# Strassen operand sums of a GNN kernel: x sums pair by pair from quarters, weight sums in three buffers

## The chip, the cores and the metric

The kernel runs on one core of a Trainium2 chip. Its engines each run a program of their own and meet at semaphores: PE multiplies matrices, ACT and DVE work elementwise on tiles and on PE's results, POOL (GpSimd) does elementwise work beside them, and SP does nothing here but issue DMAs in the order of its program. The metric is device time of one launch in microseconds (us), lower is better.

## The reference, cut to what matters

1250 nodes with 1024 features go through four graph layers on one edge list (10000 random edges both ways, and the self loops); each layer is `x = layernorm(x + layer(x))`. What the change touches are the products of x or of a layer's input with a 1024 x 1024 weight matrix in float32:

```python
# layer 0: x1 = x @ W1 + b1, then four gated graph steps on 512 columns
for kk in range(4):
    alpha = tanh(x_i @ gw[:x.shape[1]] + x_j @ gw[x.shape[1]:] + gb)
    gnn_out = gnn_out + segment_sum(norm[:, None] * alpha * x_j, col)
# layer 1: two SAGE layers, relu between them
h = relu(x @ W_self0 + (segment_sum(x[src], dst) * deg_inv) @ W_neigh0 + b0)
out = h @ W_self1 + (segment_sum(h[src], dst) * deg_inv) @ W_neigh1 + b1
# layer 2: attention; h = x @ W, e = exp(-leaky_relu(al[src] + ar[dst]))
out = elu(segment_sum(e * h[dst], src) / (rowsum + EPS))
# layer 3: GCN
out = relu(segment_sum((x @ W)[src] * norm, dst) + b)
```

## The kernel before

**Tiles and turns.** Nodes are cut into NT = 10 tiles of T = 125. schedule() (L89) lists 325 jobs, JOBS, and every engine's program is one loop over the turns j, in which it does its part of job j and of some jobs ahead: PE the matmuls of job j, ACT first() and DVE second() the operands of a job one or two turns on, SP loads of jobs three to four turns on. The jobs in order: x1 (10), the gates of layer 0 (4 x 10), then for each SAGE layer a product with the self weights ("self", 35 jobs), one with the neighbour weights ("zq", 25 and later 10 more jobs) and the graph sums ("mean", 10 and 10 half jobs); then attention (z, att, kept), the last product (zq of layer 4, 25 and 10 jobs) and its graph sums ("loop").

**Quarter products.** A self or zq product is not done as one matrix product but, for each pair of row tiles (HT = 5 pairs, tile i and tile i + 5), as seven quarter products in the manner of Strassen and Winograd, one per phase: P1, P2, P4, P6, P7, P5, P3 for self, P1, P2, P6, P7, P4, P5, P3 for zq, five jobs each. Each multiplies a quarter of x (128 x 500, as 4 pieces of 128 x 125) or a sum of quarters with a quarter of W (512 x 512) or a sum of quarters. P1, P2 and P4 use plain quarters of x; P6, P7, P5 and P3 use sums (X_SUM): with x in quarters x11, x12, x21, x22, P5 takes S1 = x21 + x22, P6 S1 − x11, P7 x11 − x21, P3 x12 − (S1 − x11). P4 to P7 use sums of W (W_SUM). The numbers are float32 split into a high and a low part (xh, xl and wh, wl), so a quarter product is 4 x 3 matmuls, L1126 to L1128.

**x on its way.** SP's load(j) (L937) brings a quarter to one of four half buffers of xs at turn j − 4; ACT's first() makes xh (L1399), DVE xl (L1762), and PE's first matmul of the job, L1126, waits for xl. Weight slabs (128 x 512) come by stage() (L818) from W or, for the sums, from ws_d in memory; ACT L1389 and DVE L1749 split them.

**The sums.** sums_schedule() (L442) lists the steps (turn, kind, product, index) in one row. All go through two large buffers in turn, PW: U3F and XB (in the rows U and XO), four quarters each. A step at turn t: SP's step_load at t − 1 (two DMAs of 512 KB; L864 for weights, L876 for x), four POOL operations in four_sums at t (L2426 to L2432 for weights, L2434 to L2440 for x), SP's step_store at t + 2 (1 MB, L883 to ws_d or L885 to xs_d), which waits for the last of the four (semaphore s_sums). The load of step n waits for the store of step n − 2 to have landed. The job's own load then reads the sum back from xs_d. The weight steps of the first product stand in the gates from turn 14 on, the x steps at the first ten turns of self1, self2 and zq4, the other weight steps in the stages of products, 2 or 3 turns apart.

```python
for n in STEP_STORE.get(j, []):    # SP, turn j
    step_store(n)
for i in LOAD_AT.get(j, []):
    load(i)
for g in STAGE_AT.get(j, []):
    stage(g)
for n in STEP_LOAD.get(j, []):
    step_load(n)
```

**Around it.** In the gates SP loads the adjacency block Ar (L962), the rows R that are added (L910) and stores ul_d (L967); POOL turns the variances of a finished tile into 1/sigma by six small operations (soon(), L2355 to L2412). In the turns of self's P5 and P3, store_right (L895) stores 125-row halves to sr_d, two buffers in turn. For mean and loop jobs, DVE's second() makes the low part of an operand (L1773 signals it) at the start of turn j − 1, in front of post() of that turn, and PE's L1270 waits for it. In "mean", second half, of layer 2 DVE also makes the two attention sums of a tile (L2003, L2006).

## Time and profile before

| | us |
|---|---|
| median of 3 runs | 1686.04 (1683.31 to 1690.53) |
| the profiled execution | 1690.04 |
| its span | 1688.2 |
| PE busy | 1521.5 (90%) |
| DVE, ACT, POOL busy | 1033.9, 800.0, 404.4 |

By stage, with the spans in which the trace has them: gates 0 and 1 from 112.9 to 265.9 us, gates 2 and 3 to 413.4, self1 to 558.9, zq1 to 657.4, mean1 to 706.9, the rest of zq1 to 737.1, mean1's second half to 789.8, self2 to 923.7, zq2 to 1025.0, mean2 and the rest of zq2 to 1101.1, mean2's second half to 1176.6, attention to 1442.3, zq4 to 1541.5, loop4 to 1620.2 and its second half to 1688.2.

A group's row reads: line, engine, operation, output and inputs, count, then busy time and mean, then the idle time of the engine ahead of these instructions and what ended it. A wait is named by what came last. In a row of the chain of waits, "DMA a<-b" is the time from the issue of a transfer to its landing; a name with q (SPq, DVEq) is the engine's instruction queue.

### The profile page before, as it was taken

To read this page: it belongs to the slowest core of one execution; us is meant where nothing else is said; L and a number is where in the kernel's file an instruction comes from. 1 tells how busy PE (TensorE), PEld (TensorE's weight loads), DVE (VectorE), ACT (ScalarE), POOL (GpSimd) and SP (SyncE) were. 2 spreads that over 40 slices of the span, in tenths; PEclk is the share of its full clock that TensorE was granted. 3 is DMA by queue.
4 is the path that set the end of the run, shared out by engine and by line. 5 is a ranking of instruction groups with operands and counts; after the bars stand their busy time and mean duration, and the time that the engine had idled before them with its cause. 6 is when DMAs were issued, how large, how long until landed. Compare 5 with 4: busy or idle time off the path is not lost.

```text
span 1688.2 us, 19851 instructions
## 1 busy us (share of the span) xinstructions
PE 1521.5 (90%) x6685; PEld 1203.4 (71%) x6685; DVE 1033.9 (61%) x1652; ACT 800.0 (47%) x1498; POOL 404.4 (24%) x457
## 2 busy tenths in 40 slices
PE   8999999999678869999779779987999999879997
PEld 6877778788456647877557558766788778657775
DVE  9878898876347445554446455556589356245655
ACT  7676657677223324544123324344487246433332
POOL 0111252434443130001451320012144013320012
PEclk9999999999889989999889889998999999989998
DMA  5343374248987664547986664356656247783435
GB/s 193 112 156 105 109 239 140 95 145 283 315 280 250 234 214 159 191 151 231 288 301 233 233 212 130 127 177 231 197 161 201 92 169 273 254 261 124 143 91 176
DMA packets 152564, 324.03 MB, mean 192 GB/s; under 512 B 27202, under 2 KB 67772, under 8 KB 149896
## 3 DMA queue, kind: packets, MB, share of 16 engines
q1 hardware_dynamic: 139486, 283.87, 51.9%
q10 hardware_dynamic: 12970, 38.77, 6.0%
q8 instruction: 61, 1.00, 0.2%
q14 instruction: 47, 0.39, 0.1%
HBM read 221.76 MB, written 100.82 MB: 191 GB/s over the span
## 4 chain that ended last, share of the span: by engine, by line
PE 41%; DMA 24%; DVE 13%; ACT 8%; POOL 6%; issue 5%; SPq 2%; ACTq 1%; DVEq 0%; POOLq 0%
PE bank L1259 8%; PE bank L1263 6%; PE bank L1261 6%; DMA Ar<-a_d 5%; DMA xs_d<-U 3%; DMA sr_d<-U 3%; PE bank L1095 3%; PE bank L1096 3%; PE bank L1097 3%; DMA xs<-xs_d 3%; PE bank L1270 3%; PE bank L1126 2%; PE bank L1127 2%; PE bank L1128 2%; ACT Tt L1434 2%
## 5 line engine op out<-in xcount | busy, mean ns | idle before, releaser
L1259 PE MATMUL bank<-Zh,Mh 125*125 125x512 f32 x990 | 401.0, 405 | 3.5 <-DVE Zl L1831 3.2
L1126 PE MATMUL bank<-wh,xh 128*125 128x512 f32 x700 | 299.7, 428 | 114.4 <-DVE xl L1762 99.1
L1762 DVE TENSOR_TENSOR xl<-xs,xh 128x500 fp32r<-128x500 f32 (+1 forms) x205 | 168.7, 823 | 340.8 <-ACT xh L1399 339.0
L1399 ACT CAST xh<-xs 128x500 fp32r<-128x500 f32 (+1 forms) x205 | 137.0, 669 | 412.8 <-DMA xs<-xs_d 185.1
L1127 PE MATMUL bank<-wl,xh 128*125 128x512 f32 x700 | 291.9, 417 | 0.0
L1128 PE MATMUL bank<-wh,xl 128*125 128x512 f32 x700 | 290.9, 416 | 0.0
L1126 PEld LDWEIGHTS bank<-wh,xh 128*125 128x125 f32 x700 | 140.4, 201 | 167.9 <-issue 126.7
L1270 PE MATMUL bank<-Zl,Mh 125*125 125x512 f32 x590 | 238.5, 404 | 19.6 <-DVEq L1773 19.5
L1259 PEld LDWEIGHTS bank<-Zh,Mh 125*125 125x125 f32 x990 | 187.3, 189 | 49.6 <-ACT Zh L1469 4.1
L1128 PEld LDWEIGHTS bank<-wh,xl 128*125 128x125 f32 x700 | 139.8, 200 | 36.9
L1127 PEld LDWEIGHTS bank<-wl,xh 128*125 128x125 f32 x700 | 140.9, 201 | 33.1
L1263 PE MATMUL bank<-Zh,Ml 125*125 125x512 f32 x400 | 158.8, 397 | 4.0 <-DVE Ml L1776 4.0
L1261 PE MATMUL bank<-Zl,Mh 125*125 125x512 f32 x400 | 158.0, 395 | 0.0
L2355 POOL TENSOR_TENSOR mv<-mv,half 125x1 f32<-125x1 f32 x39 | 38.9, 998 | 492.4 <-DVE mv L1953 492.4
L1270 PEld LDWEIGHTS bank<-Zl,Mh 125*125 125x125 f32 x590 | 112.4, 191 | 51.9 <-issue 25.5
L1434 ACT ACTIVATE Tt<-PB,Q 125x125 f32<-125x125 f32 x400 | 120.8, 388 | 1.9 <-ACT XO L1546 1.9
L1749 DVE TENSOR_TENSOR wl<-Tt,wh 128x512 fp32r<-128x512 f32 x94 | 81.9, 871 | 49.9 <-ACT wh L1389 49.9
L1416 ACT CAST Mh<-Ar 125x1250 fp32r<-125x1250 int16 x60 | 74.2, 1236 | 77.8 <-DMA Ar<-a_d 41.4
L1416 ACT CAST Mh<-Tt 125x1250 fp32r<-125x1250 f32 x53 | 65.7, 1239 | 67.9 <-DVE Tt L1790 64.4
L1095 PE MATMUL bank<-wh,xh 128*125 128x512 f32 x232 | 95.9, 413 | 1.7 <-ACT xh L1399 1.2
L1096 PE MATMUL bank<-wl,xh 128*125 128x512 f32 x240 | 95.3, 397 | 0.0
L1097 PE MATMUL bank<-wh,xl 128*125 128x512 f32 x240 | 94.5, 394 | 0.0
(228 smaller groups left out, 2567.4 us busy)
## 6 DMA issues: line engine op xcount, KB each, us to landing
Ar<-a_d SPq DMA_DIRECT2D x100, 312.5 KB, 3.0
xs<-xs_d SPq DMA_DIRECT2D x100, 250.0 KB, 5.3
x_d<-XO ACTq DMA_DIRECT2D x30, 512.0 KB, 4.4
R<-x_d SPq DMA_DIRECT2D x60, 256.0 KB
xT_d<-XT ACTq DMA_DIRECT2D x30, 500.0 KB, 4.0
Tt<-ws_d SPq DMA_DIRECT2D x52, 256.0 KB, 5.7
xs<-xT_d SPq DMA_DIRECT2D x45, 250.0 KB, 6.2
ws_d<-U SPq DMA_DIRECT2D x10, 1024.0 KB, 4.9
```

What stands on the lines that cost most here:

```text
L1095: te.matmul(o, xh[b][:, k, :], wh[s][:], start=(k == 0), stop=False)
L1096: te.matmul(o, xh[b][:, k, :], wl[s][:], start=False, stop=False)
L1097: m = te.matmul(o, xl[b][:, k, :], wh[s][:], start=False, stop=(k == 7))
L1126: te.matmul(o, xh[b][:, 4 * h + k, :], wh[s][:], start=(k == 0 and not onto), stop=False, skip_group_check=True)
L1127: te.matmul(o, xh[b][:, 4 * h + k, :], wl[s][:], start=False, stop=False, skip_group_check=True)
L1128: m = te.matmul(o, xl[b][:, 4 * h + k, :], wh[s][:], start=False, stop=(k == 3), skip_group_check=True)
L1259: te.matmul(o, Mh[i][:, s, :], zh, start=(n == 0), stop=False)
L1261: te.matmul(o, Mh[i][:, s, :], zl, start=False, stop=False)
L1263: m = te.matmul(o, Ml[i][:, s, :], zh, start=False, stop=(n == NT - 1))
L1270: m = te.matmul(o, Mh[i][:, s, :], zl, start=False, stop=(n == NT - 1))
L1434: m = ac.activation(t[:, s, :], PB[:, d, :], ACT.Tanh, bias=PQ[k % 2][1][:, s:s + 1])
L1762: ve.tensor_tensor(xl[b][:, part, :], xs[b][:, part, :], xh[b][:, part, :].bitcast(f32), ALU.subtract) \
```

## The change

x sums. The four-quarter steps for x are gone, and so is xs_d4. For each row pair there are now four small sums, S1, P6, P7 and P3, listed in XSUMS. SX holds S1 (five buffers, four in XB and one in GW), SM the others (five: UF0, UF1 and three quarters of GW). SP's sum_load brings the quarter or quarters two turns ahead of the POOL operation (three for S1 in layers 1 and 2), pair_sum on POOL makes the sum three turns ahead of its job in one operation (two for P3), and ACT and DVE read it where it is (x_of), without a load of their own. In layers 1 and 2 sum_store writes each quarter to xs_d two turns later, since the zq jobs still read the sums from there; a place of SM is loaded again when that store has landed (place_free). The loads of jobs that need another quarter go one turn earlier, five ahead.

Weight sums. A step now has a place, a load turn, four turns for its four operations and a store turn; there are three places, U3F, XB and GW. The first product's steps stand in gates 2 and 3 instead of 0 to 2; zq1's and zq2's stand over some thirty turns each, and self2's in the second half of layer 1's mean.

Two more edits: the two loads of attention's row vectors into GW go from turn 51 to turn 87, and DVE's second() for mean and loop jobs from tile 2 on stands in lower() of the turn before, behind post() of the turn before that.

```diff
-        LOAD_AT.setdefault(_j - (4 if _job.kind in ("att", "self", "zq") else 3), []).append(_j)
+        LOAD_AT.setdefault(_j - (5 if _job.phase in X_SUM and (_job.kind == "self" or _job.layer == 4) else
+                                 4 if _job.kind in ("att", "self", "zq") else 3), []).append(_j)
...
-    steps = [(J0[0] + 4 + 6 * k, "w", 0, k) for k in range(4)]
-    at = {p: find(*p, phase="P1") for p in PRODUCTS}
-    steps += [(at["self", 1] + 2 * i, "x", 1, i) for i in range(HT)]
-    steps += [(at["self", 1] + 11 + 2 * k, "w", 1, k) for k in range(4)]
...
+    g, z = LAST_GATE, START["self", 1]
+    steps = [(1, g - 16, (g - 15, g - 14, g - 13, g - 12), g - 11, 0, 0),
+             (0, g - 13, (g - 11, g - 10, g - 9, g - 9), g - 8, 0, 1),
+             (2, g - 8, (g - 7, g - 7, g - 6, g - 6), g - 5, 0, 2),
+             (0, g - 6, (g - 5, g - 5, g - 4, g - 4), g - 3, 0, 3),
+             (0, g - 2, (g - 1, g - 1, g, g), z, 1, 0),
+             (2, g - 3, (z, z + 1, z + 2, z + 3), z + 4, 1, 1),
+             (0, z + 3, (z + 5, z + 6, z + 7, z + 8), z + 9, 1, 2),
+             (0, z + 12, (z + 14, z + 15, z + 16, z + 17), z + 18, 1, 3)]
...
+XSUMS = []
+for _p in (("self", 1), ("self", 2), ("zq", 4)):
+    for _i in range(HT):
+        XSUMS.append((START[_p] + (6 + 3 * _i // 2 if _p[0] == "self" else 3 + _i), _p[1], "S1", _i))
+    for _f in ("P6", "P7", "P3"):
+        for _i in range(HT):
+            XSUMS.append((find(*_p, _i, phase=_f) - 3, _p[1], _f, _i))
...
+    XSUM_LOAD.setdefault(_t - (3 if _f == "S1" and _layer < 3 else 2), []).append(_n)
+    if _layer < 3:
+        XSUM_STORE.setdefault(_t + 2, []).append(_n)
...
+            def place_free(n):
...
+                    sum_made(q, *XSUMS[o][1:])
+                    if layer < 3 and XSUMS[o][2] != "S1":
+                        sum_stored(q, *XSUMS[o][1:])
+                        q.wait_ge(s_xl, XI[find("self", layer, i, phase=XSUMS[o][2])] + 1)
...
                 for i in LOAD_AT.get(j, []):
                     if i >= 2:
                         load(i)
+                for n in XSUM_LOAD.get(j, []):
+                    sum_load(n)
                 for g in STAGE_AT.get(j, []):
                     stage(g)
+                for n in XSUM_STORE.get(j, []):
+                    sum_store(n)
...
-                    q.wait_ge(d_xs[X_SLOT[j]], 16 * X_NTH[j])
+                    if sum_of(j) is None:
+                        q.wait_ge(d_xs[X_SLOT[j]], 16 * X_NTH[j])
+                    else:
+                        q.wait_ge(s_sx, sum_of(j) + 1)
...
-                    elif JOBS[i].kind in ("gate", "att", "kept"):
+                    elif JOBS[i].kind in ("gate", "att", "kept") or JOBS[i].kind in ("mean", "loop") and JOBS[i].d >= 2:
                         second(i)
...
+                j = find("self" if layer < 3 else "zq", layer, i, phase=f)
+                sum_made(q, layer, "S1", i)
...
+                if f == "P6":
+                    po.tensor_tensor(o, SX[i], o, ALU.subtract).then_inc(s_sx, 1)
+                    return
...
-                for n in STEP_AT.get(j, []):
-                    four_sums(n)
+                for n in XSUM_AT.get(j, []):
+                    pair_sum(n)
+                for n, m in STEP_AT.get(j, []):
+                    weight_sum(n, m)
```

SP at the start of self1, before: x steps (L876 loads, L885 stores), x loads (L937) and weight slabs (L818).

```order
L876 DMA XO<-xT_d1 128x2x500 [waits s_tt,d_xo0,d_xo1,d_ps1]
L876 DMA XO<-xT_d1 128x2x500 [waits d_xt0]
L885 DMA xs_d1<-U3 512x1x500 [waits s_sums]
L937 DMA xs1<-xT_d1 128x500 [waits s_xl]
L818 DMA ws0<-ws_d0 128x512 [waits s_wl]
L937 DMA xs1<-xT_d1 128x500 [waits s_xl]
L818 DMA ws1<-ws_d0 128x512 [waits s_wl]
L876 DMA U3<-xT_d1 128x2x500 [waits d_ps0]
```

SP in self1 where the sums of P6 are stored and those of P7 loaded, after: L1051 is sum_store, L1041 the load of a quarter for a sum, L1106 the job's load, L932 the slab; d_sq counts landed sum stores, s_sx sums made.

```order
L1051 DMA xs_d1<-GW 128x500 [waits d_sq0]
L1051 DMA xs_d1<-U0 128x500 [waits d_sq1,s_sx]
L1106 DMA xs0<-xT_d1 128x500 [waits s_xl]
L1041 DMA U0<-xT_d1 128x500 [waits d_sq1]
L932 DMA Tt1<-ws_d0 128x512 [waits s_wl]
L1051 DMA xs_d1<-U1 128x500 [waits d_sq2,s_sx]
L1106 DMA xs0<-xT_d1 128x500 [waits s_xl]
L1041 DMA U1<-xT_d1 128x500 [waits d_sq2]
L1051 DMA xs_d1<-GW 128x500 [waits d_sq3,s_sx]
L1106 DMA xs1<-xT_d1 128x500 [waits s_xl]
```

The 1 MB stores and their four-quarter loads are replaced by a store and a load of one quarter per turn; from the fourth row on a load into U0, U1 or GW stands behind the landing of the store from the same place, and the slab of a later job stands behind that.

POOL at the start of self1, before:

```order
L2434 TENSOR_TENSOR U3<-U3 128x500 [waits d_pl0]
L2436 TENSOR_TENSOR U3<-U3 128x500 [waits s_own_p]
L2438 TENSOR_TENSOR U3<-U3 128x500 [waits s_own_p]
L2440 TENSOR_TENSOR U3<-U3 128x500 [waits s_own_p]
L2434 TENSOR_TENSOR XO<-XO 128x500 [waits d_pl1]
L2436 TENSOR_TENSOR XO<-XO 128x500 [waits s_own_p]
L2438 TENSOR_TENSOR XO<-XO 128x500 [waits s_own_p]
L2440 TENSOR_TENSOR XO<-XO 128x500 [waits s_own_p]
```

POOL in self1 in the turns ahead of P6 and P7, after: L2630 makes a P6 sum, L2634 a P7 sum, L2604 to L2608 are operations of a weight step.

```order
L2630 TENSOR_TENSOR U0<-XO,U0 128x500 [waits s_sx,d_sm0]
L2630 TENSOR_TENSOR U1<-XO,U1 128x500 [waits s_sx,d_sm1]
L2630 TENSOR_TENSOR GW<-XO,GW 128x500 [waits s_sx,d_sm2]
L2604 TENSOR_TENSOR U3<-U3 128x512 [waits d_pl0]
L2630 TENSOR_TENSOR GW<-XO,GW 128x500 [waits s_sx,d_sm3]
L2606 TENSOR_TENSOR U3<-U3 128x512 [waits s_own_p]
L2630 TENSOR_TENSOR GW<-GW 128x500 [waits s_sx,d_sm4]
L2608 TENSOR_TENSOR U3<-U3 128x512 [waits s_own_p]
L2634 TENSOR_TENSOR U0<-U0,xs0 128x500 [waits d_xs0,d_sm0]
L2610 TENSOR_TENSOR U3<-U3 128x512 [waits s_own_p]
L2634 TENSOR_TENSOR U1<-U1,xs0 128x500 [waits d_xs1,d_sm1]
```

Four dependent operations on one buffer have become one per sum, with the weight operations one by one between them.

POOL in gate 3, after (L2533 to L2590 are soon(), before L2355 to L2412, which stood there alone):

```order
L2590 TENSOR_SCALAR mv<-mv 125x1 [waits s_own_p]
L2604 TENSOR_TENSOR U3<-U3 128x512 [waits d_pl0]
L2606 TENSOR_TENSOR U3<-U3 128x512 [waits s_own_p]
L2533 TENSOR_TENSOR mv<-mv,half 125x1 [waits s_post]
L2535 TENSOR_TENSOR mv<-mv 125x1 [waits s_own_p]
L2537 TENSOR_TENSOR mv<-mv 125x1 [waits s_own_p]
L2539 TENSOR_SCALAR mv<-mv 125x1 [waits s_own_p]
L2541 TENSOR_TENSOR mv<-mv 125x1 [waits s_own_p]
L2590 TENSOR_SCALAR mv<-mv 125x1 [waits s_own_p]
L2608 TENSOR_TENSOR U3<-U3 128x512
L2610 TENSOR_TENSOR U3<-U3 128x512 [waits s_own_p]
```

Two operations of a weight step now stand behind the small ones of each of two turns.

## Rows read from the trace of the kernel before

**Rows 1.** The page, part 1: engine, busy us, share, instructions.

```profile
PE 1521.5 (90%) x6685; PEld 1203.4 (71%) x6685; DVE 1033.9 (61%) x1652; ACT 800.0 (47%) x1498; POOL 404.4 (24%) x457
```

**Rows 2.** Groups by line on PE: busy us, mean ns, idle before, releasers.

```profile
L1126 PE MATMUL bank<-wh,xh 128*125 128x512 f32 x700 | 299.7, 428 | 114.4 <-DVE xl L1762 99.1 <-ACT xh L1399 11.0 <-issue 3.9
...
L1270 PE MATMUL bank<-Zl,Mh 125*125 125x512 f32 x590 | 238.5, 404 | 19.6 <-DVEq L1773 19.5
```

**Rows 3.** Windows on PE: stretch, us, busy (count), clock, DMA share, GB/s.

```profile
112.90:265.90 153.00, 146.44 (x625) 0.98 0.46 154
265.90:413.40 147.50, 146.25 (x665) 1.00 0.48 161
413.40:558.90 145.50, 115.67 (x454) 0.89 0.83 279
558.90:657.40 98.50, 78.35 (x302) 0.90 0.57 199
737.10:789.80 52.70, 50.41 (x232) 1.00 0.67 207
789.80:923.70 133.90, 109.81 (x433) 0.91 0.82 274
923.70:1025.00 101.30, 80.10 (x301) 0.88 0.57 198
1101.10:1176.60 75.50, 61.79 (x257) 0.89 0.61 206
1442.30:1541.50 99.20, 80.59 (x333) 0.91 0.71 226
536.60:561.70 25.10, 25.10 (x110) 1.00 0.69 231
```

**Rows 4.** SP's waits, 558 to 658 us: total, times, longest.

```profile
SPq L883 <- POOL XO L2432: 23.0, 2, 12.8
SPq L883 <- POOL U L2432: 21.5, 2, 11.1
```

**Rows 5.** SP's waits, 410 to 560 us.

```profile
SPq L883 <- POOL XO L2432: 12.2, 2, 9.8
...
SPq L885 <- POOL U L2440: 7.0, 2, 6.6
```

**Rows 6.** The chain of waits, 448 to 482 us: start us, us, what.

```profile
452.01 8.26 DMA xs_d<-U
...
460.86 6.99 DMA U<-xT_d
...
471.92 1.78 POOL U L2440
```

**Rows 7.** DMA issues, 196 to 345 us: KB each, us to landing.

```profile
Ar<-a_d SPq DMA_DIRECT2D x20, 312.5 KB, 3.1
...
ul_d<-U SPq DMA_DIRECT2D x10, 256.0 KB, 2.3
```

**Rows 8.** DMA issues, 440 to 475 us.

```profile
xs<-xT_d SPq DMA_DIRECT2D x7, 250.0 KB, 8.2
```

**Rows 9.** The chain of waits, 540 to 600 us.

```profile
543.68 6.51 DMA sr_d<-U
```

**Rows 10.** Windows on PE: 420 to 430 us.

```profile
420.00:430.00 10.00, 10.00 (x53) 1.00 1.00 401
```

**Rows 11.** POOL's timeline, 366 to 378 us: start, us, instruction.

```profile
374.38 0.27 POOL L2412 TENSOR_SCALAR mv<-mv 125x1 f32<-125x1 f32 x1
```

**Rows 12.** The chain of waits, 204 to 230 us.

```profile
212.76 0.43 SPq L883
...
213.74 7.57 DMA Ar<-a_d
```

**Rows 13.** The timeline of SP, 811 to 813 us.

```profile
811.58 1.80 SPq L937 DMA_DIRECT2D xs<-hT_d  x1
```

305 lines of the change are left out of this document (213 added, 92 removed).

## The prediction

> **What bounds the kernel now.** I read the page first: the matrix engine is busy 1521.5 us of the span, 90% [rows 1]. So at most 167 us can be had from waits; the matmuls themselves stay. The groups by line say where the waits are: 114.4 us stand ahead of L1126, the first matmul of a quarter product, 99.1 of them for xl, and 19.5 ahead of L1270 [rows 2]. xl is only the last link of load, xh, xl, so the question is what delays the load. The windows by stage localise it [rows 3]: the five stages made of quarter products (413.4 to 657.4, 789.8 to 1025.0, 1442.3 to 1541.5) have 115.67, 78.35, 109.81, 80.10 and 80.59 us of matmul in 145.50, 98.50, 133.90, 101.30 and 99.20 us, while the gates ahead of them (265.9 to 413.4) have 146.25 of 147.50. Where no wait falls, 110 matmuls take 25.10 us: a quarter product, 12 matmuls, is 2.79 us with the lost records filled in (nine products in that stretch). The self stages have 35 such products (97.7 us) and the zq stages 25 (69.8 us), which leaves 47.8, 28.7, 36.2, 31.5 and 29.4 us of loss, 174 in all.
>
> Two things make it. SP issues in order, so a store that waits for GpSimd holds every later load: in the zq1 stage L883 waits 23.0 + 21.5 us in four steps [rows 4], and in the self1 stage L885 and L883 wait 7.0 and 12.2 us [rows 5]. The chain shows what an x sum costs [rows 6]: 6.99 us for its quarters, four GpSimd operations until 473.70, some 8 us for the store (8.26 for the one before), and only then the load of the sum: about 21 us from quarter to sum, against 2.79 us of work per turn. Second, the granted clock is 0.88 to 0.91 of 2.4 GHz in these stages on average, where PE waits again and again, and 1.00 in the gates, the upper level throughout [rows 3]: a stall is followed by some time at the lower level.
>
> **The change, part by part.** All terms are against the profiled execution, 1690.0 us; the median of the runs is 4 us below it.
>
> *Self1, 145.5 us.* x sums no longer pass through memory before use: a GpSimd operation reads quarters that landed two or three turns ago and ACT reads the result where it lies. A 250 KB transfer takes 2.3 us on a calm queue and 8.2 on a full one [rows 7, 8], with 5.6 us (two turns) to 8.4 (three) ahead of the operation, and an operation is at most 1.78 us [rows 6] with 8.4 ahead of the product. That covers it unless the queue is full. GpSimd has 25 x, 12 weight and 5 other operations of this size in the stage, 42 x 1.8 = 76 us, so it is no bound. What stays: (a) the store of the first weight step at the stage's first turn waits for two operations of the turn before, and the load of x for a later product stands behind it: 5 us and 2 of clock, between nothing and the 7.57 us that Ar takes behind such a store today [rows 12]; (b) the next such store at the fourth turn, 3 us; (c) each P7 quarter goes into the buffer from which the P6 sum of that row is stored, and its load waits for that landing, issued only a turn earlier. This wait is new, and behind it on SP's queue stand the next weight slab and the next x load. If a landing is L, the turn is L + 1.5 us; the nearest rows are the 2.3 us of a 256 KB store in the gates and the 8.2 of a load here; I take 5, the middle, as the queue's share in this stage is 0.83, so five turns lose 5 + 1.5 − 2.79 = 3.7 each, 18, less the 8 us (three turns) of lead with which they begin: 10 us; (d) 4 us of clock; (e) 6 us for a queue near its limit, since the stage issues 113 transfers instead of 95 on SP. Together 30 of today's 47.8 remain: **−18** (bounds −40 and +5).
> *Zq1, 98.5 us.* The four weight steps that held SP 44.5 us [rows 4] become loads 10 turns ahead of their store and single operations in between: their gaps go. What remains lies in front: the stores of 125-row tiles go pairwise, each waiting for the one two earlier, and land after 6.51 us [rows 9], so 3.2 us a turn against 2.79. The change adds one 250 KB transfer in seven of these turns, 250 KB / 401 GB/s [rows 10] = 0.65 us of queue each: ten turns lose 4.5 + 4.5 = 9 us, less some 4 of lead, 5 us. With 6 us for the start of the stage, clock and the two row loads moved there: 81, **−18**.
> *Self2, 133.9 us.* As self1 but without weight steps in it and with 105 transfers for 95: loop and start, 7 us stay; **−29**. *Zq2, 101.3 us*: as zq1 without its tail of stores held up: 9 us stay, **−22**. *Zq4, 99.2 us*: sums never stored, no landing waits; the first sums come from tiles made late in the stage before, 4 us: **−25**.
> *Mean, second half of layer 2, 75.5 us.* The same ten jobs in layer 1 take 52.70 [rows 3]. Here 75.50 − 61.79 = 13.7 us stand ahead of the matmuls, most of the 19.5 that L1270 waits for L1773 [rows 2, 3]; DVE issues it a turn ahead but behind the reductions of the attention sums, and the change puts it in front of them. Next are the loads of Ar and the transposes. I take not quite half of the 22.8: **−10** (0 to −22). *Loops −4*, from the same move. *Mean, second half of layer 1, 52.7 us*: four weight steps come in, 8.4 MB on top of 207 GB/s x 52.7 = 10.9 MB: 366 GB/s against the 401 at full share [rows 10]. Nearly full: **+2** (0 to +10).
> *Gates 0, 1.* Four weight steps leave them. Today they have 153.00 − 146.44 = 6.6 us of loss [rows 3]: **−6**. *Gates 2, 3, 147.50 us with 146.25 of matmul.* They come here, with two operations per turn for three of the steps, queued behind the small operations of L2355 to L2412, which begin only when statistics arrive: in gate 3 the last of them is at 374.38, some 8 us after its turn began [rows 11]. Two operations of 1.6 to 1.8 us more end 11.4 us into the turn, while a turn is 7.8 (147.50 / 19 products of 35 matmuls). The 1 MB store at the next turn therefore holds SP 3.6 us, and Ar, needed three turns on, is issued behind it: today an Ar right behind such a store took 7.57 us [rows 12], against 3.1 for the median in the gates [rows 7]. Four steps, gaps of about 4.6, 1.5, 5 and 0: **+11** (0 to +23).
>
> Sum: −18 −18 −29 −22 −25 −10 −4 +2 −6 +11 = −119: 1571 by the profiled execution, 1567 by the median. I give **1570**.
>
> On the stores of 125-row tiles, the trace shows 6.51 us for a landing [rows 9]. The Trainium skill, "DMA: Bandwidth & Descriptors", section "Why a DMA increments its semaphore by 16 and not by 1", says that a transfer goes to as many engines as the largest number up to 16 that divides its slowest dimension, so 125 rows go to 5 engines and 128 to 16. By it an added 128-row transfer delays these stores only on 5 of the engines, by the same 0.65 us, and the sum stays; were the engines shared otherwise, the 5 us would be 0. No row separates the two.
> On small transfers, the trace has 2.3 us for 256 KB where the queue is calm [rows 7]. The same page, "Anatomy of one DMA — SWDGE (gpsimd) path", gives about 2.0 us fixed plus bytes by 436 GB/s, which speaks against this change: four stores of 250 KB pay the fixed part four times. By it a landing is an estimated 2.6 us, the loop turn 4.1, and self1 and self2 would each be about 8 us better than I have them if the queue were calm; the trace's 8.2 us on a full queue says that it is not always calm [rows 8].
>
> **The rivals.**
> *A. The queue stays full* (15%). For: landings of 8.2 us and a share of 1.00 at 420 us [rows 8, 10], 18 more transfers. Then the landing loop is 9.7 us a turn: 5 x 6.9 − 8 = 27 instead of 10, in both self stages +34; the gates at their bound +12, zq1 +10, the mean stage of layer 1 at its bound +8, zq4 +6. −119 + 70 = −49: 1641, or **1637** by the median. Against: the sums of zq4 are never stored, and the stages other than the two self stages are at shares of 0.57 to 0.71 [rows 3].
> *B. Everything is hidden* (8%). In the stretch at 2.79 us a share of 0.69 held nothing up [rows 3]. The loops (20), the gates (11) and the store at the first turn (7) fall away: −157, **1529**. Against: the loop's wait for a landing issued one turn before is in the order itself, and 2.3 us is the shortest landing there is.
> *C. Slower: SP's own issuing* (4%). 113 issues in 35 turns are 3.2 a turn; SP takes 0.43 us for one when the queue is calm [rows 12] and up to 1.80 when it is full [rows 13]. 2.79 / 3.2 = 0.87 each is where it starts to set the pace, and about 1.55 where it has eaten all that is won. At 1.7, self1 is 192 (+47), self2 3.0 x 35 x 1.7 = 178 (+45), zq1 −18, zq2 −22, zq4 87 (−12), mean −10, gates +5: +35, **1721**. For: the longest row is beyond 0.87. Against: it stands alone in its stage, and here the mean would have to be as long.
> *D. It does nothing* (3%): the same waits appear under other names, since the load of a sum's quarter still waits for xl and for a store; **1686**.
>
> **The numbers.** Forecast 70%, within 1540 to 1605 by the bounds above taken half together; A 15, B 8, C 4, D 3. 80% is held by 1530 to 1640. About 0.5% is what a measurement of this kernel can tell: faster 0.93, same 0.03, slower 0.04.
>
> **What would show it.** Right: L883/L885's successors wait under 10 us a stage; waits ahead of the quarter products fall from 114.4 us to 40 to 60; the zq stages are at 75 to 82 us, self2 near 105, self1 near 128. In self1 SP waits for the landing of a sum's store during P7, some 5 turns. In gates 2 and 3 matmuls wait for Ml behind Ar. The last ten mean jobs of layer 2 wait no longer for L1773's successor. Wrong, if landings in the self stages are 8 us throughout (A), if SP shows issues of over 0.9 us on average with no wait (C), or if gates 2 and 3 lose over 25 us.

## The result and the profile after

The changed kernel takes 1579.9 us (1576.9 to 1583.2 in four runs) against 1686.8 (1683.3 to 1690.5): a ratio of 0.937, with a 95% interval of 0.933 to 0.940. Forecast were 1570, so −116, and 1530 to 1640; measured are −107. The profiled execution took 1583.2 us, with a span of 1581.4.

One correction ahead of the readings. The steps in the second half of layer 1's mean, which the section on the change and one expectation call self2's, make the weights of zq2's product: the five groups of steps make the weights of self1, zq1, self2, zq2 and zq4, and each group stands in a stage before its product. Where they stand, which is all that the sums used, was right.

The page has PE busy 94% of the span instead of 90% [rows 1]:

```profile
PE 1484.0 (94%) x6685; PEld 1177.1 (74%) x6685; DVE 1058.0 (67%) x1652; ACT 799.5 (51%) x1498; POOL 425.6 (27%) x472
```

The same 6685 matmuls are busy for 37.5 us less (1521.5 to 1484.0). The prediction had the matmuls themselves stay and only waits go; about a third of the gain of 106.8 us of span is shorter matmuls, with the mean granted clock of the execution at 0.982 instead of 0.954.

The groups by line show the wait ahead of the first matmul of a quarter product fall from 114.4 to 34.2 us, below the 40 to 60 that were forecast. The wait for DVE's second() (L1442, before L1270) falls from 19.6 to 13.8 [rows 2]. The first matmul's mean, 428 ns before, is 405.

```profile
L1298 PE MATMUL bank<-wh,xh 128*125 128x512 f32 x700 | 283.2, 405 | 34.2 <-DVE xl L1938 21.5 <-ACT xh L1574 4.6 <-issue 4.1
```

The windows by stage answer rows 3 (stretch, us, PE busy and matmuls, granted clock, DMA share, GB/s): gates 0 and 1; gates 2 and 3; self1; zq1; the second half of layer 1's mean; self2; zq2; the second half of layer 2's mean; zq4; the last ten zq4 jobs.

```profile
113.00:256.30 143.30, 142.75 (x625) 1.00 0.38 120
256.30:418.50 162.20, 150.90 (x664) 0.97 0.55 196
418.50:533.60 115.10, 104.21 (x453) 0.99 0.86 306
533.60:613.40 79.80, 72.68 (x301) 0.98 0.68 238
693.10:757.40 64.30, 54.78 (x228) 0.92 0.78 264
757.40:863.60 106.20, 101.63 (x433) 0.98 0.79 266
863.60:944.40 80.80, 73.85 (x301) 0.96 0.65 222
1020.60:1089.80 69.20, 59.00 (x254) 0.93 0.64 221
1358.60:1434.00 75.40, 73.85 (x334) 1.00 0.63 217
1481.70:1514.30 32.60, 28.97 (x120) 1.00 0.34 107
```

| stage | before | forecast | after |
|---|---|---|---|
| gates 0, 1 | 153.0 | −6 | 143.3 (−9.7) |
| gates 2, 3 | 147.5 | +11 | 162.2 (+14.7) |
| self1 | 145.5 | −18 | 115.1 (−30.4) |
| zq1 | 98.5 | −18 | 79.8 (−18.7) |
| mean of layer 1, second half | 52.7 | +2 | 64.3 (+11.6) |
| self2 | 133.9 | −29 | 106.2 (−27.7) |
| zq2 | 101.3 | −22 | 80.8 (−20.5) |
| mean of layer 2, second half | 75.5 | −10 | 69.2 (−6.3) |
| zq4 | 99.2 | −25 | 75.4 (−23.8) |
| loops | 118.1 | −4 | 114.7 (−3.4) |
| all other stages | | 0 | +7 |

The loops are loop4 without the last ten zq4 jobs, which stand between its halves.

Of SP's waits in zq1, L883's successor (L979) is gone; SP waits for a free x buffer instead, so its issues are ahead of what the engines use:

```profile
SPq L1106 <- DVE xl L1938: 32.7, 17, 5.0
```

In self1 this sign did not come: L979 waits 17.9 us there, 15.0 of it at the store of the stage's first turn.

In the second half of layer 2's mean PE's wait for DVE's second() went from 13.7 to 1.4 us, as forecast. But 8.6 us of waits for ACT (L1782) stand there now, which the kernel before does not have, so the stage gave 6.3 us instead of 10.

### The profile page after: what moved, and what is told of

It is laid out like the page before. It is cut to its first block, busy times and chain, and to the rows that moved or that the text cites. A ratio compares the mean times of both kernels' runs of the same rounds, so it can differ in the third digit from the quotient of the medians.

```text
span 1581.4 us, 20003 instructions
## 1 busy us (share of the span) xinstructions
PE 1484.0 (94%) x6685; PEld 1177.1 (74%) x6685; DVE 1058.0 (67%) x1652; ACT 799.5 (51%) x1498; POOL 425.6 (27%) x472
## 4 chain that ended last, share of the span: by engine, by line
PE 52%; DMA 19%; DVE 11%; ACT 7%; issue 5%; POOL 3%; SPq 2%; ACTq 0%; DVEq 0%; POOLq 0%
PE bank L1431 10%; PE bank L1435 6%; PE bank L1433 6%; DMA Ar<-a_d 5%; PE bank L1442 4%; PE bank L1298 4%; PE bank L1300 4%; PE bank L1299 4%; DMA sr_d<-U 4%; PE bank L1267 3%; PE bank L1268 3%; PE bank L1269 3%; ACT Tt L1609 2%; DMA xs<-xT_d 2%; DMA R<-sr_d 1%
## 5 line engine op out<-in xcount | busy, mean ns | idle before, releaser
L1298 PE MATMUL bank<-wh,xh 128*125 128x512 f32 x700 | 283.2, 405 | 34.2 <-DVE xl L1938 21.5
L1300 PE MATMUL bank<-wh,xl 128*125 128x512 f32 x700 | 278.7, 398 | 0.0
L1299 PE MATMUL bank<-wl,xh 128*125 128x512 f32 x700 | 278.6, 398 | 0.0
L1442 PE MATMUL bank<-Zl,Mh 125*125 125x512 f32 x590 | 237.9, 403 | 13.8 <-DVEq L1949 13.5
L1938 DVE TENSOR_TENSOR xl<-xs,xh 128x500 fp32r<-128x500 f32 (+1 forms) x160 | 140.2, 877 | 159.4 <-ACT xh L1574 158.6
L1574 ACT CAST xh<-xs 128x500 fp32r<-128x500 f32 (+1 forms) x160 | 109.7, 687 | 188.0 <-DMA xs<-xT_d 63.2
L1298 PEld LDWEIGHTS bank<-wh,xh 128*125 128x125 f32 x700 | 131.0, 187 | 79.0 <-issue 37.4
L1300 PEld LDWEIGHTS bank<-wh,xl 128*125 128x125 f32 x700 | 131.7, 188 | 33.8
L1299 PEld LDWEIGHTS bank<-wl,xh 128*125 128x125 f32 x700 | 131.7, 188 | 31.1
L1442 PEld LDWEIGHTS bank<-Zl,Mh 125*125 125x125 f32 x590 | 112.3, 190 | 44.6 <-issue 18.4
L2533 POOL TENSOR_TENSOR mv<-mv,half 125x1 f32<-125x1 f32 x39 | 39.1, 1002 | 303.2 <-DVE mv L2131 303.2
L1925 DVE TENSOR_TENSOR wl<-Tt,wh 128x512 fp32r<-128x512 f32 x94 | 88.5, 942 | 42.1 <-ACT wh L1561 42.1
L1966 DVE TENSOR_TENSOR Tt<-Tt,Ar 125x1250 f32<-125x1250 f32 (+2 forms) x48 | 67.9, 1419 | 46.2 <-ACT Tt L1609 32.9
L1591 ACT CAST Mh<-Tt 125x1250 fp32r<-125x1250 f32 x53 | 65.7, 1239 | 64.3 <-DVE Tt L1966 62.5
L1267 PE MATMUL bank<-wh,xh 128*125 128x512 f32 x232 | 96.6, 416 | 0.9 <-ACT xh L1574 0.9
L1268 PE MATMUL bank<-wl,xh 128*125 128x512 f32 x240 | 95.9, 400 | 0.0
```

The source lines that it names most:

```text
L1267: te.matmul(o, xh[b][:, k, :], wh[s][:], start=(k == 0), stop=False)
L1268: te.matmul(o, xh[b][:, k, :], wl[s][:], start=False, stop=False)
L1298: te.matmul(o, xh[b][:, 4 * h + k, :], wh[s][:], start=(k == 0 and not onto), stop=False, skip_group_check=True)
L1299: te.matmul(o, xh[b][:, 4 * h + k, :], wl[s][:], start=False, stop=False, skip_group_check=True)
L1300: m = te.matmul(o, xl[b][:, 4 * h + k, :], wh[s][:], start=False, stop=(k == 3), skip_group_check=True)
L1442: m = te.matmul(o, Mh[i][:, s, :], zl, start=False, stop=(n == NT - 1))
```

## Experiments

The kernel before was timed beside each group of runs. Its median was 1686.8 us beside the changed kernel, 1690.1, 1694.6 and 1693.7 beside three groups of runs, and 1686.8 beside the last one. A difference between the medians of two groups can therefore be off by some 8 us. Where that matters, the difference of the ratios (of 1686.8 us) is given with it. Stage lengths are from windows of one profiled execution each; a stage's boundaries are those of its first and last job.

### DVE's second() put back

```diff
-                    elif JOBS[i].kind in ("gate", "att", "kept") or JOBS[i].kind in ("mean", "loop") and JOBS[i].d >= 2:
+                    elif JOBS[i].kind in ("gate", "att", "kept"):
...
-                if j + 1 < NJ and JOBS[j + 1].kind in ("mean", "loop") and JOBS[j + 1].d < 2:
+                if j + 1 < NJ and JOBS[j + 1].kind in ("mean", "loop"):
```

> The changed kernel, with DVE's second() for mean and loop jobs back at the start of the turn before, as in the kernel before. If this move is what took 6.2 us off the second half of layer 2's mean stage and some 1 to 3 us off each loop stage (theory), those stages go back to about 75.5, 50 and 68 us and the time is 8 to 12 us longer, about 1590. Rival: these stages became shorter because less is left in the DMA queue or on SP when they begin; then the time stays within 3 us of the changed kernel's 1579.9. The first half of layer 1's mean stage (49.5 us, no waits) should not change by either.

Measured: 1602.1 us (ratio to the kernel before 0.947, 0.942 to 0.952), 22 us longer by the medians and 17 by the ratios, more than the 8 to 12 expected. The windows of the second halves of layer 1's and of layer 2's mean:

```profile
704.20:771.30 67.10, 55.33 (x231) 0.92 0.77 261
1030.40:1107.90 77.50, 61.93 (x257) 0.89 0.60 202
```

Layer 2's second half goes up by 8.3 us (77.5 against 69.2), loop4 by 2.3 and the two halves of layer 1's mean by 2.7 and 2.8; zq1 is 5.8 longer in its trace as well. So the move is worth 16 of the 107 us in the stages in which it acts (8.3 + 2.3 + 2.7 + 2.8). The expectation had the place right but called the first half of layer 1's mean immune, since the kernel before has no wait there. The kernel before stands at 49.5 us in it with the same DVE order; what is new there is a weight step with its POOL operations and its store, which I take for the cause; no run tested it. Why zq1 is longer is open: nothing in it or ahead of it was changed, but SP waits 9.9 us for landings of sr_d stores there instead of 5.4. A zq stage of one profiled execution can thus differ by this much.

### Weight steps of zq1 and zq2 close together again

```diff
-        steps += [(1, z, (z + 3, z + 4, z + 5, z + 6), z + 7, p, 0),
...
+        steps += [(1 - k % 2, z + 1 + 3 * k, (z + 2 + 3 * k,) * 4, z + 4 + 3 * k, p, k) for k in range(4)]
```

> The changed kernel, with the weight steps of zq1 and zq2 three turns apart again: load one turn ahead, all four POOL operations in one turn, store two turns after, the next x loads behind the store. x sums stay as changed. Theory: these steps held SP and made nearly all the loss of the two stages (98.5 and 101.3 us before, 79.8 and 80.8 after), so each goes back up by 15 to 20 us: about 1612 to 1620. Rival: zq gained because the queue arrives emptier from the self stages or because of one turn more of lead; then the step placement is worth under 10 us in all, under 1590.

Measured: 1633.4 us (0.965, 0.960 to 0.970): 53 us longer (48 by the ratios), more than expected. The windows are zq1 and zq2; under them SP's waits in zq1.

```profile
533.20:638.60 105.40, 79.99 (x301) 0.92 0.60 210
887.90:992.80 104.90, 80.72 (x301) 0.89 0.58 201
```

```profile
SPq L976 <- POOL U L2607: 21.4, 2, 11.0
SPq L976 <- POOL XO L2607: 20.8, 2, 10.8
```

The waits of rows 4 are back, 21.4 + 20.8 us against 23.0 + 21.5, and the stages are at 105.4 and 104.9 us, longer even than before (98.5 and 101.3). The rival falls: with the x sums as changed, putting the weight steps back alone takes zq back, and their placement (turns of load, operations and store together) is worth 25.6 and 24.1 us.

### The kernel before without x steps

```diff
-    steps += [(at["self", 1] + 2 * i, "x", 1, i) for i in range(HT)]
...
-    steps += [(at["self", 2] + 2 * i, "x", 2, i) for i in range(HT)]
...
-    steps += [(at["zq", 4] + 2 * i, "x", 4, i) for i in range(HT)]
...
-                    if job.phase in X_SUM:
-                        step_stored(q, STEP_OF["x", job.layer, job.d])
-                        src = xs_d[job.layer][job.d][:, X_SUM[job.phase], :]
-                    else:
-                        r, f = X_QUARTER[job.phase]
+                    if True:
+                        r, f = X_QUARTER.get(job.phase, (0, 0))
```

> The kernel before with its fifteen x steps left out (no four-quarter loads, no sums of x, no 1 MB stores); the phases P6, P7, P5 and P3 multiply the plain quarter x11 in place of a sum, so the output is not the reference's. Weight steps as before. Theory: in self1, self2 and zq4 the loss came from the x steps, so they fall to what the changed kernel has, about 115 to 120 (a weight step still holds SP there), 106 to 112 and 73 to 76 us, while zq1 and zq2 stay near 98 and 101: about 1605. Rival: weight steps made half of the loss of the self stages (SP waited 12 to 17 us for them there); then self1 and self2 stay above 125 and 115 us and the time is above 1625.

Measured: 1602.1 us (0.945, 0.942 to 0.948). Self1, zq1, self2, zq4:

```profile
414.10:521.60 107.50, 103.35 (x453) 0.98 0.82 282
521.60:623.10 101.50, 80.00 (x301) 0.90 0.57 196
754.40:860.10 105.70, 101.17 (x433) 0.98 0.75 253
...
1380.20:1453.40 73.20, 73.20 (x333) 1.00 0.54 171
```

Against rows 3 self1 falls by 38.0, self2 by 28.2, zq4 by 26.0 us, while zq1 and zq2 (860.1 to 961.4) stand at 101.5 and 101.3. The x steps made all but 10 of the 47.8 us of self1, and the weight steps there make little without them, although SP waits for them.

Zq4 has no weight steps in either kernel, and the changed one is within 3 us of the one without x sums (75.4 against 73.2): there the sums are hidden. Self2 is not so clean a comparison. It stands at 106.2 against 105.7, but the kernel without x steps still has zq2's weight steps in self2, and the changed kernel has none there. SP waits 15.1 us for their POOL operations (L880) and PE 4.5 us for xl, in three waits around the twentieth job. So self2's x sums, which are also stored, may cost some us that this comparison hides. Self1 has 7.6 us more, with weight steps in both kernels.

### Self1's weight steps back in the gates 1 and 2

```diff
-    steps = [(1, g - 16, (g - 15, g - 14, g - 13, g - 12), g - 11, 0, 0),
-             (0, g - 13, (g - 11, g - 10, g - 9, g - 9), g - 8, 0, 1),
-             (2, g - 8, (g - 7, g - 7, g - 6, g - 6), g - 5, 0, 2),
-             (0, g - 6, (g - 5, g - 5, g - 4, g - 4), g - 3, 0, 3),
+    steps = [(0, g - 33, (g - 32, g - 31, g - 30, g - 29), g - 27, 0, 0),
+             (1, g - 29, (g - 28, g - 27, g - 26, g - 25), g - 23, 0, 1),
+             (0, g - 24, (g - 23, g - 22, g - 21, g - 20), g - 18, 0, 2),
+             (1, g - 19, (g - 18, g - 17, g - 16, g - 15), g - 13, 0, 3),
```

> The changed kernel, with the four weight steps of the first product back in gates 1 and 2 (loads at turns 16, 20, 25, 30, one operation per turn, stores two turns after the last operation); the two that follow stay at turns 46 to 54. Theory: gates 2 and 3 lost 14.7 us because a store waits on SP for POOL operations that stand behind the small ones of gate 3, and Ar and R loads behind it: that goes to at most 3 us, apart from the gap of 8 us in the last gate job, which comes from the 2 MB of the next two steps; the gates gain 6 to 8 us and the time is about 1572. Rival 1: the bytes are what costs, wherever they stand: gates 0 to 2 lose what gate 3 gains, within 3 us of 1579.9. Rival 2: the last gap goes as well, about 1565.

The first load into XB also waits for the pads that are written at the start (s_pad), here and wherever steps start this early.

Measured: 1569.7 us (0.928, 0.923 to 0.933), 10 us less (15 by the ratios). Gate 1 and gate 3:

```profile
185.00:261.60 76.60, 71.85 (x311) 1.00 0.61 207
332.20:407.50 75.30, 75.30 (x354) 1.00 0.66 229
```

Gate 3 has no wait left (75.30 of 75.30; it was 91.6 us long), gate 1 has 76.6 for 70.9. The theory had the 8 us gap of the last gate job stay, because it was put down to the bytes of the next two steps; it went although those steps stand where they were. So rival 2 is right on that gap, and rival 1 holds in part: gate 1 pays 5.7 us. The changed kernel's trace shows why: SP's waits at 326 to 420 us, and the chain into the gap.

```profile
SPq L979 <- POOL U L2610: 25.6, 2, 15.0
SPq L979 <- POOL GW L2610: 14.7, 1, 14.7
```

```profile
388.43 2.42 POOL U L2610
...
396.84 9.79 DMA R<-ul_d
```

SP stood at the store of the fourth step until POOL's last operation ended (388.43 + 2.42), issued it at 390.86, and then had six more transfers to issue ahead of R (Ar, x and four of weights); R landed 9.79 us after its issue, and DVE and PE waited for it. So the late store and the bytes behind it make this gap together.

### The same stores one turn later

```diff
-    steps = [(1, g - 16, (g - 15, g - 14, g - 13, g - 12), g - 11, 0, 0),
-             (0, g - 13, (g - 11, g - 10, g - 9, g - 9), g - 8, 0, 1),
-             (2, g - 8, (g - 7, g - 7, g - 6, g - 6), g - 5, 0, 2),
+    steps = [(1, g - 16, (g - 15, g - 14, g - 13, g - 12), g - 10, 0, 0),
+             (0, g - 13, (g - 11, g - 10, g - 9, g - 9), g - 7, 0, 1),
+             (2, g - 8, (g - 7, g - 7, g - 6, g - 6), g - 4, 0, 2),
```

> The changed kernel, with the stores of the first three weight steps (gates 2 and 3) one turn later and nothing else moved: the same bytes and the same POOL operations. Theory: what costs in gate 3 is SP standing at a store whose POOL operation is not done while Ar and R wait behind it; one turn later the operation is done, the waits of 14.7 us and of most of the 25.6 us go, and gate 3 loses 3 of its three gaps but not the last: about 91.6 to 84 us for gate 3, about 1573. Rival: POOL operations or bytes cost by themselves; nothing changes, within 3 us of 1579.9.

Measured: 1578.3 us (0.932, 0.930 to 0.935), within noise of the changed kernel; but gate 3 is at 86.4 us instead of 91.6:

```profile
327.70:414.10 86.40, 78.20 (x354) 0.94 0.73 260
```

```profile
SPq L979 <- POOL U L2610: 20.4, 2, 12.4
...
SPq L979 <- POOL GW L2610: 6.4, 1, 6.4
```

The wait for GW's operations fell from 14.7 to 6.4 us and that for U's from 25.6 only to 20.4, most of it the fourth step, which was not moved. 5 of the 15 us are therefore the waits at the first three stores. I take the rest for the fourth store and what is queued behind it; this run does not show it by itself.

### zq2's weight steps spread out

```diff
-            steps += [(1, z + 44, (z + 45, z + 45, z + 46, z + 46), z + 47, 3, 0),
-                      (0, z + 46, (z + 47, z + 47, z + 48, z + 48), z + 49, 3, 1),
-                      (1, z + 49, (z + 50, z + 50, z + 51, z + 51), z + 52, 3, 2),
-                      (0, z + 51, (z + 52, z + 52, z + 53, z + 53), z + 54, 3, 3)]
+            steps += [(1, z + 33, (z + 35, z + 36, z + 37, z + 38), z + 39, 3, 0),
+                      (1, z + 40, (z + 42, z + 43, z + 44, z + 45), z + 46, 3, 1),
+                      (1, z + 47, (z + 49, z + 50, z + 51, z + 52), z + 53, 3, 2),
+                      (0, z + 52, (z + 54, z + 55, z + 56, z + 57), z + 58, 3, 3)]
```

> The changed kernel, with the four weight steps of self2 spread from turn 118 to 143 instead of 129 to 139. Theory: the second half of layer 1's mean stage lost 11.7 us because 8.4 MB in ten turns fill the queue, so that loads of R land after 9 to 13 us; spread out, the stage goes back to 55 to 58 us and the end of zq1, whose queue is at a share of 0.34, hides the first: about 1573. Rival: the waits come from DVE's instruction order (L1949 behind L2300) and stay: within 3 us of 1579.9. Third possibility: self2's first jobs lose what the mean stage gains, since a step now stands there.

Measured: 1576.5 us (0.933, 0.927 to 0.939), which by itself is within noise of the changed kernel. The end of zq1 and the second half of layer 1's mean:

```profile
662.40:696.70 34.30, 30.69 (x134) 1.00 0.48 166
696.70:750.20 53.50, 51.84 (x231) 0.97 0.80 262
```

The mean stage goes back from 64.3 to 53.5 us, so its 11.6 us came from the steps that stood there. The changed kernel's chain there has:

```profile
713.76 12.82 DMA R<-in_W
...
731.75 9.87 DMA R<-in_W
```

R<-in_W is a slab of the attention layer's weights (256 KB), which DVE reduces (L2300) ahead of the second() of a mean job (L1949), for which PE waits 8.2 us. The load at 731.75 was issued just behind the two 512 KB loads of a weight step (728.43 to 731.32). The run moved bytes and POOL operations together, so it does not show that the bytes alone did it; the chain names the landings. That DVE's order makes the loss is excluded by this run, which kept the order. But the end of zq1 takes 34.3 us instead of 30.2, which the expectation took for hidden. The timelines of DVE and POOL at its end (start us, us, instruction):

```profile
685.10 0.68 DVE L2005 TENSOR_TENSOR Zl<-U,Zh 125x512 fp32r<-125x512 f32 x1
...
687.58 1.28 DVE L1938 TENSOR_TENSOR xl<-xs,xh 128x500 fp32r<-128x500 f32 x1 [1.20 <-ACT xh L1574]
688.78 1.76 DVE L2005 TENSOR_TENSOR Zl<-U,Zh 125x512 fp32r<-125x512 f32 x1
690.47 0.67 DVE L2090 TENSOR_TENSOR U<-U,bank 125x512 f32<-125x512 f32 x1
```

```profile
688.40 1.60 POOL L2606 TENSOR_TENSOR XO<-XO 128x512 f32<-128x512 f32 x1
```

This is no matter of DMA. DVE makes three operations per job here; Zl takes 1.76 us instead of 0.68 as soon as POOL works beside it (from 687.03 on), and xl 1.28 us instead of the same 0.68, while the operation that reads a PE bank keeps its 0.67. In each turn DVE also waits 1.20 us for ACT's xh. So a turn, from one xl to the next, goes from 3.08 us (684.50 to 687.58) to 4.76 (687.58 to 692.34), against the job's 2.79 us of matmuls.

### Sum stores issued twice

```diff
+    xx_d = dram("xx_d", (HT, 128, 4, QX), f32)
...
                 sy.dma_start(xs_d[layer][i][:, to, :], (SX if f == "S1" else SM)[i]).then_inc(d_sq[m % 4], 16)
+                sy.dma_start(xx_d[i][:, to, :], (SX if f == "S1" else SM)[i]).then_inc(d_sq[m % 4], 16)
```

> The changed kernel, with each of the forty small sum stores of self1 and self2 issued twice, the second to a memory of its own, and waits that take both: 5 MB per stage and 20 issues more on SP in each. Theory by my sum: a landing is then a transfer longer (some 0.65 us of queue and 0.5 us of issue on about 5.5), so the five turns of the landing loop lose 1 us each more and the rest 2 to 3 us: self1 and self2 5 to 8 us longer each, about 1593. Rival A (the queue is at its limit): 5 MB at 400 GB/s come in full, 12 us in each stage or more, over 1602. Rival (there is room): under 3 us each, below 1585.

Measured: 1599.7 us (0.944, 0.942 to 0.947), 20 us longer by the medians and 13 by the ratios. Self1, zq1, self2:

```profile
420.00:542.20 122.20, 109.14 (x453) 0.94 0.90 325
542.20:626.10 83.90, 73.75 (x301) 0.96 0.68 234
770.10:878.90 108.80, 102.17 (x432) 0.98 0.87 299
```

Self1 is 7.1 us longer, as the theory had it; self2 only 2.6, which is the rival's "under 3". The zq stages behind them, which have no doubled store, are 4.1 and 2.3 longer (zq2, from 878.9 on, takes 83.1). That the queue hands its lag on to them would explain it, but is not shown: in the first run zq1 was 5.8 us longer with nothing changed ahead of it. Neither stage pays the 12 us that 5 MB take at 400 GB/s, so neither queue is full throughout, as rival A had it. In self1 the share of DMA is 0.86 without them and 0.90 with them, in self2 0.79 and 0.87: self1's queue has the less room.

### P7's sums a turn later

```diff
-            XSUMS.append((find(*_p, _i, phase=_f) - 3, _p[1], _f, _i))
+            XSUMS.append((find(*_p, _i, phase=_f) - (2 if _f == "P7" and _p[0] == "self" else 3), _p[1], _f, _i))
```

> The changed kernel, with the P7 sums of self1 and self2 made two turns ahead of their job instead of three, and so loaded and stored one turn later: the load of a P7 quarter then stands two turns behind the store from the same buffer. Theory: SP's waits for landings of sum stores in P6 and P7 (12.4 us in self1, 13.9 in self2) fall to under 3, and the gaps of 2.6 and 1.0 us ahead of self1's last two P7 jobs go, since the queue is no longer late: self1 3 to 5 us shorter, self2 1, about 1575. Rival: the turn of lead that the sum loses costs as much; P7 jobs wait for their sum instead, 1580 or more.

Measured: 1583.8 us (0.934, 0.931 to 0.937): by the ratio not to be told from the changed kernel. Self1 is 116.7 us, 1.6 longer, where 3 to 5 less were expected. SP's waits for landings of sum stores ahead of these loads fell, as expected (L1041, from 12.4 to 2.0 us). In the changed kernel the landing loop is on the chain at the fourth P7 job: the store of a P6 sum, and the load into its buffer.

```profile
485.97 3.15 DMA xs_d<-GW
...
489.14 4.65 DMA GW<-xT_d
```

With the sums later, that wait is gone from the chain, but the gaps stay (2.1 and 0.9 us at the same two jobs). POOL's timeline shows what is late next:

```profile
490.33 1.26 POOL L2634 TENSOR_TENSOR GW<-GW,xs 128x500 f32<-128x500 f32 x1 [3.61 <-DMA GW<-xT_d]
494.24 1.31 POOL L2646 TENSOR_TENSOR G<-U,G 125x512 f32<-125x512 f32 x1 [2.64 <-DVE U L2050]
495.50 1.24 POOL L2634 TENSOR_TENSOR GW<-GW,xs 128x500 f32<-128x500 f32 x1
```

L2646, an addition that waits for the DVE operation of the present job, now stands ahead of each P7 sum on POOL. One wait was changed for another; on the stage the rival is right.

### Steps moved: three versions

The first puts self1's steps into gate 2, zq1's first two a few turns earlier, and three of zq2's steps into self2. The second spreads self1's from turn 22 and takes zq2's as in the spread version; the third has self1's from turn 16. The places of the six first steps in the second version:

```diff
+    steps = [(0, g - 27, (g - 25, g - 24, g - 23, g - 22), g - 20, 0, 0),
+             (1, g - 23, (g - 21, g - 20, g - 19, g - 18), g - 16, 0, 1),
+             (0, g - 19, (g - 17, g - 16, g - 15, g - 14), g - 12, 0, 2),
+             (1, g - 15, (g - 13, g - 12, g - 11, g - 10), g - 8, 0, 3),
+             (0, g - 10, (g - 9, g - 8, g - 7, g - 6), g - 4, 1, 0),
+             (2, g - 7, (g - 5, g - 4, g - 3, g - 2), g, 1, 1),
```

> The changed kernel, with steps moved by what the runs showed: the four steps for self1's weights between turns 28 and 40 (gate 2, where POOL has one operation a turn), the two that follow at turns 39 to 49 with a store two turns after the last operation, and of the four for zq2's weights one in the mean stage's second half and three in self2, one POOL operation a turn. Theory: gate 3 goes from 91.6 to 76 to 78 us and gate 1 keeps its 71, self1 loses the gaps at its fifth and ninth job (6 us), the mean stage goes from 64.3 to 54 to 56, self2 pays 2 to 5 us: about 1552. Rival: self2 pays what the mean stage gains, since its queue is the fullest: about 1560.

Measured: 1570.0 us (0.927, 0.924 to 0.930). Self2:

```profile
736.90:851.10 114.20, 104.19 (x432) 0.97 0.81 280
```

The mean stage gains 11.1 us (683.7 to 736.9) and self2 pays 8.0 of it, so the rival is right on that; but the time is above the rival's 1560 too (1564 by the ratio). Gate 2, at 70.6 us in the changed kernel, takes 75.3 (256.9 to 332.2) with two POOL operations a turn in it.

> The changed kernel, with only step times moved: self1's four weight steps from turn 22 to 41 with one POOL operation a turn, the next two at turns 39 to 49, zq2's four at turns 118 to 143. By the stages of the runs so far: gate 3 77 to 79 us instead of 91.6, gate 1 3 us longer, self1 4 shorter, the mean stage 10 shorter, the end of zq1 4 longer: about 1557. Rival: the gaps seen in gate 1 with steps there (2.5 and 2.0 us) come wherever a step stands in a gate, so two more in gate 2: about 1564.

Measured: 1559.1 us (0.920, 0.916 to 0.923), near the expected 1557. One operation a turn costs gate 2 nothing (257.7 to 328.6, 70.9 us), and gate 3 is at 77.1.

> As the run before, but self1's four weight steps from turn 16 to 36, where they cost 5.7 us in gate 1 and nothing in gates 2 and 3. By the stages of the runs so far, −16 for gate 3, +6 for gate 1, −4 for self1, −11 for the mean stage, +4 for the end of zq1: −21, about 1559. Rival: the two steps at turns 39 to 49 bring back a store that holds SP in gate 3, +5: 1564.

Measured: 1566.8 us (0.925, 0.922 to 0.928), above the rival's 1564 by the median and at the expected 1559 by the ratio (1560), with gate 1 at 75.8 us, near the 76.6 of the run with the same places. By its profiled execution (span 1560.5) it is 4 us behind the second version, by its median 8; the gates account for 2, and the rest is open.

### The first loads of zq1 and zq2 later

This comes on top of the second of the three versions.

```diff
-        steps += [(1, z, (z + 3, z + 4, z + 5, z + 6), z + 7, p, 0),
-                  (1, z + 10, (z + 13, z + 14, z + 15, z + 16), z + 17, p, 1),
+        steps += [(1, z + 6, (z + 7, z + 8, z + 9, z + 10), z + 11, p, 0),
+                  (1, z + 12, (z + 14, z + 15, z + 16, z + 17), z + 18, p, 1),
...
-                if j == START["zq", 1] + 2:
+                if j == START["zq", 1] + 9:
```

> The run of steps from turn 22 on (1559.1 us) with one thing more: the 1 MB of weight quarters that zq1 and zq2 load at their first turn, and the 1 MB of row vectors at zq1's third, come at their seventh and tenth turn. Theory: the gap of 3.5 us and the jobs of 8 to 9 us at the sixth job of both stages come from a load of x that lands after 9.6 us behind these 2 MB (1 MB in zq2), while the turns before are paced by the sr_d stores: zq1 goes from 80.6 to 75 to 77 and zq2 from 79.6 to 75 to 77, about 1551. Rival: SP's lag from the sr_d stores alone makes the gap; both stages stay within 1 us.

Measured: 1549.7 us (0.918, 0.915 to 0.920), 30 us less than the changed kernel (32 by the ratios). Against the second version it is 9 us less by the medians but 3 by the ratios, whose intervals overlap; that the later loads help is seen in the stages. Zq1 and zq2:

```profile
517.90:593.60 75.70, 71.13 (x301) 1.00 0.73 250
837.40:912.20 74.80, 71.15 (x302) 1.00 0.70 240
```

They fall from 80.7 and 79.6 to 75.7 and 74.8, which excludes the rival. The chain of the changed kernel at zq1's gap shows both halves of the cause: a 125-row store whose landing SP waits for, and then a load of x that lands late. Of the 2 MB that the expectation puts ahead of this load, 1 MB was issued 2.2 us ahead of it (541.86) and the other 1 MB directly behind it (544.48).

```profile
535.92 7.79 DMA sr_d<-U
...
544.10 9.60 DMA xs<-xT_d
```

## Why the prediction was right, point by point

**The bound and its two causes.** Right, and now separated. Without x steps the kernel before is 88 us faster by its profiled spans (1600.6 for 1688.2), and 92 in self1, self2 and zq4; putting back the weight steps of two stages costs 53 (48 by the ratios), and 50 in zq1 and zq2. The prediction read both from SP's in-order waits [rows 4 to 6]. The granted clock, its second point, went from 0.88 to 0.91 up to 0.96 to 1.00 in the five product stages.

**Self1, −18 forecast, −30 measured.** The step that was mis-sized is the residue of 30 us: it is 17. (a) The store at the first turn holds SP, as described, until 426.86, and costs 2.5 us of wait at the fifth job instead of 5. (b) The store at the fourth turn did not hold SP; it was issued at 436.62 straight behind the loads ahead of it. The 3.54 us of wait at the ninth job, which takes 8.1 us, have another cause. The load of x for it, issued at 437.15 behind 2 MB (two loads of 512 KB and that store of 1 MB), landed 12.1 us later, on a full queue. The stretch from 436 to 452 us, and its loads of x with their median landing:

```profile
436.00:452.00 16.00, 12.42 (x52) 0.98 1.03 400
```

```profile
xs<-xT_d SPq DMA_DIRECT2D x5, 250.0 KB, 12.1
```

So (e), the queue near its limit, did come, in one place: 5.3 us over the job's 2.79, where 6 were forecast for the stage and 3 for (b). (c) The landing loop: 10 forecast, 4 measured (5.7 and 4.1 us for two jobs of 2.79). SP does wait for landings in five turns, 7.7 + 4.7 us in all, and the wait on the chain is 3.15 us where I took 5; the loop's turn is then 4.7, five turns lose 9, and the 8 us of lead absorb nearly all. The mechanism was there and the middle of 2.3 and 8.2 was too high.

**Zq1, −18; zq2, −22; self2, −29; zq4, −25.** Measured −18.7, −20.5, −27.7, −23.8. In zq1 the pace of the 125-row stores came as described: jobs 1 to 4 take 3.7 to 3.9 us. What the prediction put at 6 us for start, clock and row loads is the sixth job of 8.0 us, which the last run shows to come from the 2 MB that are loaded early. The same first load costs zq2 5 us, which the prediction had not named there, and which its 9 us of residue held by luck.

**Mean of layer 1, second half: +2 with a bound of +10, measured +11.6.** The step that failed. The sum asked whether 366 GB/s fit under 401 and found that they do, nearly; the right question was how long the loads that the stage waits for take to land when they do. The slabs R<-in_W took 12.82 and 9.87 us on the chain, with a lead shorter than that. The measured rate was 264 GB/s in the stretched stage, so the mean rate never was the limit.

**Gates 2 and 3: +11, measured +14.7.** Right in mechanism: the store waits for POOL operations behind soon(), and Ar and R wait behind the store. The largest gap was put at the third step (5 us) and is at the fourth and R: "about 4.6, 1.5, 5 and 0" should have had 8 to 10 us at the end.

**Gates 0 and 1: −6, measured −9.7**: the prediction took idle time only. Idle time fell by 6.0 us (6.56 to 0.55), and busy time by 3.7 (146.44 to 142.75), at a granted clock of 1.00 instead of 0.98.

**DVE's move: −14 (−10 and −4), worth 16.** The two stages named went down by 6.3 and 3.4. In layer 2's second half the 13.7 us of wait that the sum read were there and went to 1.4, but 8.6 us of another wait took their place. The put-back run shows that the move also covers the two halves of layer 1's mean (2.7 and 2.8), which the other edits would have made slower. A put-back prices an edit with the others in place, and the forecast priced it against the kernel before.

**Not named at all**: the last ten zq4 jobs, 28.7 to 32.6 us. Their P3 sums, two POOL operations each, stand beside DVE's work: Zl takes 1.75 us at 1490.79 instead of 0.74, and xl 1.11 at 1489.76 instead of 0.68. No run moved these sums, so that they are the cause is argued from the timeline.

**Rivals.** A (1637) needed 8.2 us of landing throughout; the median in self1's P6 and P7 is 4.5 for a sum store, and landings reach 8 us and more in self1's first jobs, in the mean stage of layer 1 and in the last gate. B (1529) fails at the same places. C: SP's issues in self1 take 0.52 us on average (110 in the stage; the longest 3.99, on the full queue), under the 0.87 at which they would set the pace. D is excluded.

On small stores the Trainium skill, "DMA: Bandwidth & Descriptors", section "Anatomy of one DMA — SWDGE (gpsimd) path", gave an estimated 2.6 us. Its figures are for transfers that GpSimd issues, and those here are SP's. The trace has 3.15 in the wait on the chain, somewhat above it, and a median of 4.5 at a queue share above 0.8, so the load of the queue counts for as much as the fixed part.

## What to carry to other kernels

A chain "load, compute, store, load again" on one in-order DMA queue costs more than its own time, because every unrelated load behind the waiting store is late; make the operand where it is consumed and let the store be a by-product, and the stage can become nearly as fast as without the work (here zq4, to within 3 us; the self stages, where the sums are stored as well, keep some us more). Where a step must be stored, put at least two turns between the last operation and the store, one operation a turn beside other work, and keep its bytes away from turns that load operands with little lead: moving only such turns gave another 30 us. When a step is moved to a quieter place, ask for the landing time of the loads that it will precede there, not for the mean rate.
